# Graph network kernel, 64 graphs on one core: the store of the output rows is issued two places later in the DMA queue's step

## The reference, cut to what matters

```python
h = jnp.maximum(_layernorm(x, axis=-1), 0.0)
x = x + _L0_gnn_ref(adj, h, W1, att_src1, att_dst1, b1, W2, att_src2, att_dst2, b2)
h = jnp.maximum(_layernorm(x, axis=-1), 0.0)
x = x + _L1_gnn_ref(h, adj, Wq, Wk, Wv, Wo)   # q, k, v, softmax over the mask, relu(out) @ Wo
return x                                      # (64, 128, 256) f32
```

## Time and profile before

| | us |
|---|---|
| median of 3 runs | 763.97 (763.64 to 764.99) |
| profiled execution, its own time | 768.98 |
| span of the profiled execution | 767.1 |
| PE busy | 716.1 (93%) |
| DVE busy | 684.1 (89%) |
| ACT busy | 592.6 (77%) |
| POOL busy | 536.5 (70%) |
| DMA queue of SP, share of 16 engines | 58.1% |

### The profile page before, as it was taken

How to read it: one execution, slowest core, us unless ns; L and a number is a source line. 1 busy time by engine, 2 the same in 40 slices (tenths; PEclk the granted TensorE clock), 3 DMA queues, 4 the chain that set the end, 5 groups by cost and what they waited for, 6 DMA issues and landing times.

```text
span 767.1 us, 26536 instructions
## 1 busy us (share of the span) xinstructions
PE 716.1 (93%) x8398; PEld 592.9 (77%) x8398; DVE 684.1 (89%) x2017; ACT 592.6 (77%) x1865; POOL 536.5 (70%) x733
## 2 busy tenths in 40 slices
PE   0689999999999999999999999999999999999973
PEld 0477788888878888888888888888887888888852
DVE  5878999999999999999999999999998999999772
ACT  0368888888877888887888888878887788788852
POOL 6558777777667677767777777677776767776651
PEclk9999999999999999999999999999999999999996
DMA  7123466756666565676566566665575556555574
GB/s 198 41 53 67 99 114 112 112 122 122 109 111 113 117 116 115 114 121 113 112 118 119 115 115 115 109 119 112 125 116 103 113 108 115 116 119 98 86 117 96
DMA packets 270423, 84.70 MB, mean 110 GB/s; under 512 B 242896, under 2 KB 269904, under 8 KB 270288
## 3 DMA queue, kind: packets, MB, share of 16 engines
q1 hardware_dynamic: 269856, 82.24, 58.1%
q10 hardware_dynamic: 432, 0.79, 0.5%
HBM read 15.86 MB, written 8.39 MB: 32 GB/s over the span
## 4 chain that ended last, share of the span: by engine, by line
PE 65%; DVE 13%; DMA 7%; issue 6%; SPq 4%; ACT 4%; POOL 1%; DVEq 0%; POOLq 0%; ACTq 0%
PE bank L928 24%; PE bank L954 8%; PE bank L1104 6%; PE bank L1064 5%; DMA hT<-h_split 5%; PE bank L1083 3%; PE bank L1045 3%; PE bank L1053 3%; PE bank L980 3%; DVE top L848 2%; SPq L297 2%; SPq L273 2%; ACT e L554 2%; PE bank L1006 1%; PE bank L1004 1%
## 5 line engine op out<-in xcount | busy, mean ns | idle before, releaser
L554 ACT ACTIVATE e<-bank,nmx,q_power 128x128 f32<-128x128 f32 x512 | 194.6, 480 | 5.1 <-DVE nmx L853 4.9
L408 POOL CAST e_split<-e 128x512 f16<-128x512 f32 x128 | 89.7, 701 | 116.7 <-ACT e L554 116.7
L410 POOL TENSOR_TENSOR e_split<-e,e_split 128x512 f16<-128x512 f32 x128 | 152.2, 1189 | 10.3
L954 PE MATMUL bank<-w,h1T 128*128 128x258 f32 x512 | 122.6, 381 | 0.0
L422 POOL TENSOR_TENSOR rstd<-var,minus_half 128x1 f32<-128x1 f32 x128 | 71.7, 560 | 66.4 <-DVE var L718 66.4
L928 PE MATMUL bank<-w_split,hT 128*128 128x260 f16 x768 | 98.2, 278 | 11.6 <-DMA hT<-h_split 6.3
L954 PEld LDWEIGHTS bank<-w,h1T 128*128 128x128 f32 x512 | 96.5, 190 | 15.7 <-DVE h1T L749 1.6
L505 ACT ACTIVATE eT<-lr,nmx 128x128 f32<-128x128 f32 x256 | 102.6, 456 | 0.8 <-DVE nmx L805 0.8
L928 PE MATMUL bank<-h2T,proj_split 128*128 128x128 f16 x1536 | 96.2, 219 | 1.5 <-DMA h2T<-h_split 1.5
L928 PEld LDWEIGHTS bank<-h2T,proj_split 128*128 128x128 f16 x1536 | 90.8, 98 | 3.7 <-DMA h2T<-h_split 2.1
L928 PEld LDWEIGHTS bank<-w_split,hT 128*128 128x128 f16 x768 | 71.1, 98 | 23.7 <-DMA hT<-h_split 8.3
(11 more groups left out here) (120 smaller groups left out, 1905.6 us busy)
## 6 DMA issues: line engine op xcount, KB each, us to landing
x_in<-in_x_dram SPq DMA_DIRECT2D x64, 128.0 KB, 2.4
out_dram<-x_out SPq DMA_DIRECT2D x64, 128.0 KB, 2.0
adj_in<-in_adj_dram SPq DMA_DIRECT2D x64, 64.0 KB, 2.4
e3T<-e_split SPq DMA_TRANSPOSE x128, 3.1
hT<-h_split SPq DMA_TRANSPOSE x64, 2.4
h2T<-h_split SPq DMA_TRANSPOSE x64, 2.5
attT<-att_split SPq DMA_TRANSPOSE x64, 2.7
w<-in_L_gnn_W_dram SPq DMA_DIRECT2D x2, 256.0 KB, 6.1
```

The lines of the kernel that those rows point to most:

```text
L408: pool.tensor_copy(e3_split[:, g.two, half, 0], e).then_inc(s[high_set], 1)
L410: pool.tensor_tensor(e3_split[:, g.two, half, 1], e, e3_split[:, g.two, half, 0], ALU.subtract).then_inc(s[low_set], 1)
L554: ins = act.activation(e3[:, g.two, h, :], S[:, h // 4, (h % 4) * N:(h % 4 + 1) * N], ACT.Exp, bias=nmx3[:, g.two, h:h + 1], scale=q_power ...
L954: ins = pe.matmul(X2[:, 0:D + 2], h1T[:, g.two, k * F:(k + 1) * F], w2[:, k, :], start=k == 0, stop=k == H - 1)
```

## The change

One entry of SP's list moves. The store of graph t - 11 is issued behind `norm1_transpose` and `e3_transpose_first`, and ahead of the two loads. It was issued behind `att_transpose`.

```diff
             steps(lambda graphs: run([
-                (e3_transpose_last, 9), (att_transpose, 10), (store, 11), (norm1_transpose, 3), (e3_transpose_first, 8),
+                (e3_transpose_last, 9), (att_transpose, 10), (norm1_transpose, 3), (e3_transpose_first, 8), (store, 11),
                 (load_adj, 1), (load_x, 0), (norm2_transpose, 6),
             ], graphs))
```

## The result

The changed kernel takes 761.81 us (median of 20 runs, 760.96 to 763.33). The kernel before, timed beside it, takes 765.17 us (20 runs, 761.96 to 766.46). The ratio is 0.996, with a 95% interval of 0.9951 to 0.9969: 3.4 us faster. The direction is as forecast and 761.81 us lies inside the range, near its upper end, but the gain is about half of the predicted one.

The account below looks back on a forecast made before the run. PE was taken as the bound, losing 9.1 us to stalls on hT. Profiled: 768.98 - 8.0 + 0.1 = 761.1 us; for the median, the middle of 756.0 and about 760, 758.0 us, range 755.0 to 762.5 us.

Parts of the forecast that it names:

- The bound and the mechanism: PE bounds at 10.89 us a step; its stalls on late hT, 9.1 us over 46 steps, can be won.
- hT is issued earlier: On SP, hT directly follows attT, 0.62 to 0.67 us earlier; its slack grows from 0.77 to about 1.4 us.
- the rival in which it lands late in every step: On SP's queue, hT directly behind attT lands late and PE waits every step: 790 us at 4.4 us landing; chance 0.04.
- What that is worth: PE's stalls in the 46 steps: between 6.5 and 9.1 us won, 8.0 us taken.
- Those 3.2 us go entirely: Loss in some ten steps with a long issue or late attT in front of hT, all of it to vanish.
- an earlier `hT` leaves the places that hurt it: In the five late-landing steps, instruction-queue packets keep their places in PE's program and miss the earlier hT; reason for 8.0 us.
- The five steps of 5.9 us: Steps where hT lands late (3.2 to 5.1 us), losing 0.7 to 1.9 us each; 3.3 to 5.9 us won.
- The choice between the profile and the median: Unprofiled median: 756.0 us if the 5.0 us lie elsewhere, about 760 if profiling adds such stalls; middle 758.0 chosen.
- My own sign of being wrong: For the whole kernel: the prediction is wrong if the profile shows the gain and the median does not.
- The moved store, the loads, h2T: Later on SP: the store's delay costs nothing; loads and h2T come 0.6 us later, covered; cost 0, bound 0.5 us.
- two signs off: On SP: e3T's first half waits for POOL in nearly every step; the wait before h2T shrinks from 1.5 to 0.9 us.
- The end: In the last steps the store just fits ahead of e3T's last half; cost 0 to 0.1 us, 1.4 if its issue is long.

Follow-up runs that it names:

- e6: The changed kernel run again with no edit: 761.09 us, ratio 0.9959 to the kernel before.
- e3: The changed kernel with hT's transpose also moved ahead of attT's: 759.89 us, ratio 0.9948 to the kernel before.
- e7: The kernel before with hT's transpose ahead of attT's and the store left behind attT: 759.70 us, ratio 0.994 to the kernel before.
- e2: The kernel before with the store one place later only, between hT's transpose and the first half of e3T: 760.66 us, ratio 0.9957.
- e4: The kernel before with load_adj also issued ahead of hT's transpose, behind the store: 772.67 us, ratio 1.0109 to the kernel before.

## Why the prediction was right, and where it was wrong

**The bound and the mechanism: right.** PE's own step of 10.89 us is the median step in every kernel here. The waits for `hT` are what the change removes: 7.9 to 1.4 us, "under 2 us" as forecast. Slack and time go together over six orders of the list: slack of about 0.28, 0.77, 1.4 and 2.35 us gives ratios of 1.011, 1, 0.996 and 0.995 or 0.994.

**hT is issued earlier: right.** 1.28 us from `attT` was forecast as 1.24 to 1.3. In undisturbed steps it lands in 2.4 us, so the rival in which it lands late in every step did not come in. Something of it did: late landings became more frequent, as the third point below says.

**The failed step is "What that is worth", the term of 8.0 us.** Measured are 3.4 us, and 3.0 in e6. Three things were wrong in the term.

First, it was read from one execution with a loss of 9.1 us, and that execution was not the usual one: three more have 5.6, 6.7 and 6.3 us, 6.2 on average. From those to the changed kernel's 3.3 is 2.9 us, from all four 3.6.

Second, I gave all of the loss to `hT`, but 1.4 us remain in e3 and e7, where PE never waits for it. They were never open to the change: in the first profile 9.1 - 1.4 = 7.7 us were, in a usual execution 6.2 - 1.4 = 4.8.

Third, "Those 3.2 us go entirely" and the reason for the choice of 8.0, that an earlier `hT` leaves the places that hurt it, did not hold. By its landing (rounded to a tenth, and counted from the start of its issue), `hT` took 3.0 us or more in 12 of the 46 steps before and in 22 now. Where the store's long issue had delayed `hT`, now `hT`'s own issue is the long one: it takes 1.5 us or more in 15 of these 22, in 6 of the 12 before. The new slack absorbed most of it, but not all. The five steps of 5.9 us keep 1.7 us; their gain of 4.2 lies inside the 3.3 to 5.9 that I gave them. The other 3.2 us keep 1.6. Of these 3.3 us, 1.4 are what e3 has too and 1.9 are still `hT`, in six steps with landings of 3.8 to 4.4 us. So 5.8 us went in the first profile, and 2.9 from a usual execution.

**The choice between the profile and the median: the wrong middle.** I set 756.0 (the 5.0 us lie elsewhere) against about 760 (they are stalls of this kind, which the profile adds) and took the middle. The second reading was nearer: most of the 5.0 us were such stalls, but of this one execution and not of profiling as such. Its forecast, a gain of 4.1 us at most and 760 us, is close to the result. My own sign of being wrong, that the profile shows the gain and the median doesn't, came half true: 6.8 us in the span, 3.4 in the median. That 761.81 lies in the range owes something to the range's width, because its upper end came from setting the 5.0 us against the lower bound.

**The moved store, the loads, h2T: right in effect, with two signs off.** SP waits for POOL before the first half of `e3T` in 29 steps, not in nearly every one: in 15 of the 46 steps `hT`'s own issue takes over 1.6 us, and there SP comes to `e3T` when its source is ready. The wait before `h2T` did not shrink to 0.9 us: it is 68.9 / 47 = 1.5 us. In an undisturbed step it is 552.32 - 550.54 = 1.8 us. It costs nothing, and e2 and e7 confirm that the store's new place is neither good nor bad in itself.

**The end: right.** The store fits between the halves of `e3T`.

**The 1.4 us that remain** are in the same steps, with nearly the same sizes, in every kernel in which no stall on `hT` covers them: 0.2 us in the 18th step of all eleven profiles, for one, and 0.1 us in each of the last four in e3. Part is a wait of PE for DVE; e3 has it like this:

```profile
PEld bank L988 <- DVE ab_split L761: 0.9, 3, 0.3
```

Why these steps are longer is not tested.

## What to carry to other kernels

In an in-order DMA queue, what matters is which issues stand in front of the one transfer that is needed in the same step; put that one as early as its source allows (here ahead of `attT` too), and the rest in any order behind it. Delays that hit only some steps make slack worth something even where the undisturbed step is covered, but they vary with the execution, so the value is a mean over executions. One profile that lies outside the spread of the plain runs is an outlier: profile again before anything is summed, and compare step by step; what is in one execution alone is no part of the usual gain.

## What was not expected of the hardware

About once a step something holds up SP's transfers by 1 to 2 us, and it drifts through the step. It shows either as a long issue (1.95 us instead of 0.57) or as a late landing (4.4 instead of 2.4 us), and which transfer it hits depends on the order of the list: with two issues between `attT` and `hT` (e4), `hT` landed late (3 us or more) in only 3 of 46 steps, while PE waited more than ever, because what stood in front was held up.

The packets on the instruction queues go with it closely. I took the first 2.4 us behind each issue of `hT`, for the 46 steps of all eleven profiles. In 256 cases no such packet was under way, and none of these landed later than 2.6 us. In 158 cases one of queue q8 was under way, and 146 of these landed after 3.0 us or more (rounded). With one of q14 alone it was 23 of 92. All 325 long issues of SP in the same stretches (over 0.4 us above the usual) had such a packet beside them; of the 3646 others, 721 had. The changed kernel has a q8 packet in this window in 22 steps and the kernel before in 9, which matches the increase in late landings. This is still an association: that the packet is the cause was not shown, since no run took these packets away.
